# A twelve-stage decoder on one core: two mixtures of experts in eight batches of four token tiles instead of four batches of eight

## The reference, cut to what matters

```python
# layer 1: softmax router, top 2 of 8, plus a shared MLP
def _mlp(x, w1, b1, w2, b2):
    h = jax.nn.gelu(jnp.einsum('bsd,di->bsi', x, w1) + b1)
    return jnp.einsum('bsi,id->bsd', h, w2) + b2
...
# layer 3: the same without the shared MLP; the two gates are the
# softmax over the two best logits; an expert has room for 1280 tokens
```

## Time and profile before

| what | before |
|---|---|
| median of 3 runs | 2355.95 us (2353.13 to 2364.38) |
| the profiled execution's own time | 2360.56 us |
| its span, first to last instruction | 2358.8 us |
| mean granted TensorE clock | 0.854 |
| PE / DVE / ACT / POOL busy | 76% / 57% / 47% / 31% of the span |
| f1, first instruction to the phase behind it | 996.8 to 1288.5 us |
| f3, first instruction to the end | 2066.4 to 2358.8 us |

### The profile page before, as it was taken

The page is one execution under the profiler, slowest core; times in us unless marked ns, Lnnn a source line. Parts: engine busy times, 40 slices in busy tenths (PEclk is TensorE's granted clock), DMA queues, the critical chain, the costliest instruction groups (busy, mean ns, idle before and its releaser), DMA issues. The chain is left out here.

```text
span 2358.8 us, 39307 instructions
## 1 busy us (share of the span) xinstructions
PE 1786.9 (76%) x14513; PEld 1229.5 (52%) x14513; DVE 1350.3 (57%) x3525; ACT 1103.6 (47%) x2265; POOL 730.6 (31%) x617
## 2 busy tenths in 40 slices
PE   3887562899987986778994886888788778851994
PEld 1554441545544664555994553655455535551774
DVE  2888578512235764554343467974399789851223
ACT  3676440333345766633442345763366566610441
POOL 1223201270463221155453003221222132156453
PEclk9888785699997998879997787999798878855997
DMA  4111272136615001112674001000000010012224
GB/s 152 82 83 83 86 246 58 28 98 165 177 48 213 33 2 55 29 38 99 213 236 154 1 1 36 29 10 10 3 2 2 2 45 24 6 40 69 64 80 137
DMA packets 143729, 173.18 MB, mean 73 GB/s; under 512 B 20913, under 2 KB 118897, under 8 KB 142609
## 3 DMA queue, kind: packets, MB, share of 16 engines
q1 hardware_dynamic: 123956, 129.09, 17.4%
q0 software_dynamic: 13248, 28.21, 3.5%
q10 hardware_dynamic: 6336, 13.37, 1.5%
HBM read 126.84 MB, written 79.05 MB: 87 GB/s over the span
## 5 line engine op out<-in xcount | busy, mean ns | idle before, releaser
L2770 POOL DMA_INDIRECT f_back<-f_ys,f_row x158 | 151.2, 957 | 173.7 <-DVE f_ys L2931 144.4
L871 PE MATMUL a_AV<-a_vx,a_pT 128*64 128x18 f32 (+1 forms) x3072 | 115.0, 223 | 42.3 <-DVE a_att L548 16.3
L2763 POOL DMA_INDIRECT f_slots<-f_pay,f_slot x128 | 124.5, 972 | 66.0 <-issue 38.2
L871 PEld LDWEIGHTS a_AV<-a_vx,a_pT 128*64 128x64 f32 x3072 | 105.9, 146 | 71.1 <-issue 36.7
L733 ACT ACTIVATE a_e<-a_e 128x512 f32<-128x512 f32 x192 | 110.2, 622 | 67.6 <-DVE a_e L563 67.6
L858 PE MATMUL a_TP<-ident,a_e 128*128 128x128 f32 x768 | 110.2, 288 | 19.0 <-ACT a_e L733 18.4
L738 ACT COPY a_pT<-a_TP 128x512 f32<-128x512 f32 x192 | 103.7, 588 | 41.9 <-PE a_TP L858 41.7
L858 PEld LDWEIGHTS a_TP<-ident,a_e 128*128 128x128 f32 x768 | 91.4, 148 | 57.5 <-ACT a_e L733 45.8
L847 PE MATMUL a_S<-a_kbd,a_qT 64*64 64x512 f32 x768 | 118.3, 693 | 0.9 <-issue 0.6
L563 DVE TENSOR_TENSOR a_e<-a_S,a_mx 128x1024 f32<-128x1024 f32 x96 | 117.3, 1221 | 2.9
L560 DVE TENSOR_REDUCE a_mx<-a_S 128x16 f32<-128x1024 f32 x66 | 80.8, 1224 | 42.8 <-PE a_S L847 41.6
(11 more groups left out here) (481 smaller groups left out, 4611.8 us busy)
## 6 DMA issues: line engine op xcount, KB each, us to landing
f_wt<-in_f_ew SPq DMA_DIRECT2D x39, 584.0 KB
f_slots<-in_blank SPq DMA_DIRECT2D x1, 18576.0 KB
f_wt<-in_f_leaf SPq DMA_DIRECT2D x94, 98.0 KB, 2.0
f_pay<-f_back SPq DMA_DIRECT2D x8, 1024.0 KB, 5.6
f_xs<-f_slots SPq DMA_DIRECT2D x47, 144.0 KB
memory_x_k<-w_stage ACTq DMA_DIRECT2D x24, 256.0 KB, 3.1
f_slots<-in_blank SPq DMA_DIRECT2D x1, 5760.0 KB
f_xs<-leaf_slots SPq DMA_DIRECT2D x22, 256.0 KB, 3.6
```

What stands on the lines that cost most here:

```text
L871: last = pe.matmul(AV[64 * c:64 * c + 64, 2 * hp * W1:2 * (hp + 1) * W1], pT[:, hp, 64 * c:64 * c + 64], vx[:, g % 2, t, c, 2 * hp:2 * hp ...
L2763: pool.indirect_dma_start(out=slots[:, :], out_offset=bass.IndirectOffsetOnAxis(ap=slot[:, c, t:t + 1], axis=0), in_=pay[:, c, t, :], in_o ...
L2770: pool.indirect_dma_start(out=back[:, :], out_offset=bass.IndirectOffsetOnAxis(ap=row[:, i % RR, t:t + 1], axis=0), in_=ys[:, i % RY, t, : ...
```

## The change

`BT` becomes 4 and `NBAT` 8, for both mixtures. What follows from it:

- `choose`, `place`, `norm_stats`, `root`, the scatters, the loads back, the adds and the stores work on four tiles at a time, eight times.
- `turn_x` fills one PSUM bank for a batch and takes the two in turn. `take_turned` copies one bank.
- In f1 all eight shared blocks now stand inside the routing batches, and none behind them. This follows from the loop bounds, not from an edit.
- POOL takes the root of batch b + 3 behind the scatters of batch b, for b = 0 to 4.
- `scale` returns without work for a tile number of four or more, so the links of `choose` that carried tiles 4 to 7 carry none.

```diff
-    BT, NBAT = 8, NT // 8
+    BT, NBAT = 4, NT // 4
...
-    x_turned, xT_ready, logits = ph.counter("x_turned", 2), ph.counter("xT_ready", 2), ph.counter("logits")
+    x_turned, xT_ready, logits = ph.counter("x_turned"), ph.counter("xT_ready"), ph.counter("logits")
...
-                if b == 0:
-                    root(3)
+                if b + 3 < NBAT:
+                    root(b + 3)
...
             def scale(b, j):
-                if b >= NBAT:
+                if b >= NBAT or j >= BT:
                     return
...
             def take_turned(b):
-                for n in range(2):
-                    act.wait_ge(x_turned.sem, x_turned.after(b, n + 1))
-                    if b and not shared:
-                        act.wait_ge(logits.sem, logits.after(b - 1))
-                    act.copy(xTall[:, 2 * b + n if shared else n, :], PJ[:, n, :]).then_inc(xT_ready.sem, 1)
+                act.wait_ge(x_turned.sem, x_turned.after(b))
+                if b >= 2 and not shared:
+                    act.wait_ge(logits.sem, logits.after(b - 2))
+                act.copy(xTall[:, b if shared else b % 2, :], PJ[:, b % 2, :]).then_inc(xT_ready.sem, 1)
...
             def turn_x(b):
                 pe.wait_ge(xn_ready.sem, xn_ready.after(b))
-                for n in range(2):
-                    if b:
-                        pe.wait_ge(xT_ready.sem, xT_ready.after(b - 1, n + 1))
-                    for t in range(4):
-                        last = pe.transpose(PJ[:, n, P * t:P * t + P], pay[:, 0, BT * b + 4 * n + t, 0:P], k.ident[:, :])
-                    last.then_inc(x_turned.sem, 1)
+                if b >= 2:
+                    pe.wait_ge(xT_ready.sem, xT_ready.after(b - 2))
+                for t in range(BT):
+                    last = pe.transpose(PJ[:, b % 2, P * t:P * t + P], pay[:, 0, BT * b + t, 0:P], k.ident[:, :])
+                last.then_inc(x_turned.sem, 1)
```

More of the change, by code:

```diff
@@ L3013, in make_logits @@
                     pe.wait_ge(logits_taken.sem, logits_taken.after(b - 1))
[L3014 to L3019, removed]
+                pe.wait_ge(xT_ready.sem, xT_ready.after(b))
+                for t in range(BT):
+                    last = pe.matmul(LG[:, E * t:E * t + E], xTall[:, b if shared else b % 2, P * t:P * t + P], router[:, :],
+                                     start=True, stop=True)
                 last.then_inc(logits.sem, 1)
```

## The result

| what | before | changed |
|---|---|---|
| median | 2355.52 us (2353.13 to 2364.38, 4 runs) | 2387.60 us (2380.00 to 2390.61, 4 runs) |
| ratio, 95% interval | | 1.0116, 1.0090 to 1.0141 |
| the profiled execution | 2360.56 us | 2385.51 us |
| its span, mean granted clock | 2358.8 us, 0.854 | 2383.7 us, 0.851 |
| f1, first instruction to the next phase | 291.7 us | 323.4 us |

The change makes the kernel slower by 1.2%: 32.1 us between the medians. In the two profiles the difference is 24.95 us: +31.7 in f1, -4.4 in f3, and -2.4 over the ten phases that were not touched. Forecast were +25.5 in f1 (26.6 less 1.1) and -7.5 in f3.

A forecast was written before the change was run, and what follows sets the result against it. It took f1 to be held by a ring over DVE, ACT and PE through the shared blocks, f3 by POOL's scatters. +26.6 - 1.1 - 5.9 - 1.6 = +18.0 us, forecast 2375 us, range 2362 to 2388.

The forecast's parts named there:

- First batch, first turn: f1: four tiles' norm, router and choice give places 9 us earlier; then 13.6 us to the next batch's places.
- Second to fifth turn: f1, from one batch's places to the next through a shared block, with a later batch's norm: 17.35 us each.
- Sixth and seventh turn: f1, last two steps from places to places: 16.0 us with no norm left, 15.4 with no transposes either.
- half clock throughout: Rival, chance 0.06: PE stays at 1.2 GHz through second layer and `place`; 20 us over four of seven turns, 2394.
- the clock spares the gelus: Rival, chance 0.15: little besides the slow-clock gelu step costs time; six turns 1.2 us shorter, 7 us in all, 2366.
- End of f1: f1, last places to expert transposes: scatters, 5.2 us to transposes, 2 for weights; experts start 26.6 us later in all.
- weights in the way: f1's end: first four weight loads stand ahead of the slots in SP's queue; between 0 and 4.04 us, taken as 2.
- f3's first scatter: f3's start: fewer tiles bring POOL's first scatter 8.9 us forward from 24.35 us; bounds 4.9 and 12.2.
- Roots: f3: five smaller roots among POOL's scatters at 0.9 us each, 4.6, replace one of 1.59; net 3.0 us more.
- f3's adding back: f3's end: last batch's two adds at half size save 1.1 us, the smaller last store 0.5; 1.6 us less.
- the ring doesn't close: Rival, chance 0.08: DVE and ACT run ahead, POOL paces f1 at 11.0 us a turn; 2343, faster below mean turn 13.8.
- Tables: f1: gelu table load of 1.28 us in each turn, without a drain; four more turns carry 5.1 us of it.

The follow-up runs named there:

- experiment 1, f1 alone: Kernel before, with four-tile batches in f1 alone and f3 as before: 2494.42 us, ratio 1.0017 to the kernel before on the same chip.
- Experiment 2: Changed kernel, but ACT makes block b's gelus ahead of the Exp of batch b + 1: 2465.35 us (0.9916 of the kernel before), again 2469.70 us (0.9925).
- experiment 6: Changed kernel, but f1 ranks on logits, both gates from one Exp; gelus first, two weight loads ahead of slots: 2464.25 us, 0.9895 of the kernel before.

## Why the prediction was right, and which terms were off

Forecast 2375 us (2362 to 2388), slower; measured 2387.6: direction and mechanism right, the time 0.5% low. The change itself was sized too small: the sum said +18.0, the profiles show +24.95, and the medians lie 32.1 apart, 1.8 times the sum. The measured time lies 0.4 us inside the range, and that it does is partly luck. The terms that were mis-sized are the last two turns, the end of f1 and the adding back of f3; the 7 us between the profiles' difference and the medians' are the place of the two profiled executions among their runs.

- *First batch, first turn:* places at 14.8 where 14.7 was forecast, 13.8 for 13.6. *Second to fifth turn:* 17.35 each forecast, 69.4 in all; measured 69.3. The ring with its norm was understood.
- *Sixth and seventh turn:* 16.0 and 15.4 forecast, 17.2 and 16.6 measured, +2.4. I took the norm's 1.4 us off and let the clock be, and the slow stretch lay on the second layer (5.92 and 5.97 us for 3.84), which cost 2.1 a turn and gave 1.0 back in the first layer. The rival "half clock throughout" named the cost and the rival "the clock spares the gelus" the gain; each came in two turns, neither in the number of turns it was priced for.
- *End of f1:* transposes 8.8 us behind the last scatter, where 5.2 and 2 for the weights were forecast: the term **weights in the way**, 2 us, was near 3.6 here; the two experiments with two loads ahead gave 1.2 and 2.75 us back, counted from the last scatter, so four loads are worth some 2.4 to 5.5 if the cost goes by their number, which no run shows. Its upper bound of 4.04 held.
- *DVE free to copy at once*, -1.1: measured -0.7. *Adding back in f1*, -1.1: measured -1.9, but the expert part took 2.1 us more. Of this the first `hide` is 1.5: behind 11.43 us without work PE ran it at a granted clock of 0.54, 3.5 us for 2.0 at full clock before. 0.6 stays unexplained.
- *f3's first scatter:* -8.9, as forecast. *Roots:* +3.7 for +3.0. Experts -4.9 for -5.9. POOL did not wait for slots.
- *f3's adding back*, -1.6: measured -0.15, from the last scatter of results to the end (24.02 us before, 23.87 now); the experts ahead of it took 0.7 more, unexplained. This step failed: I made the last batch's adds shorter, but that stretch is bounded by the DMA engines (349 GB/s), not by DVE. The window of before would have shown it.
- *The rivals.* That the ring doesn't close was the way to a faster kernel, decided at a mean turn of 13.8. The measured mean of 16.7 was above it; with gelus ahead of the Exp it is 14.0, and that kernel was faster than before on the chip where it ran.
- *Tables.* Turns 2 to 7 show the load of 1.28 us with 0.02 and 0.01 us around it, and turns 2 to 5 came out to the sum with that price. The Trainium skill, "ScalarE: Activation LUTs", section "What ACT_TABLE_LOAD costs", would add 1.38 us of drain to each switch; no row here shows it. Its section "Table sets: the hidden batching unit" speaks against such a change, and the time agrees in sign. Experiment 2 refines it for this kernel: two loads more, placed where ACT has slack, and the experts of f1 start 18 to 20 us earlier.

What stays open: where the result was measured the kernels of experiments 2 and 6 were not run. f1 of the changed kernel has the same turns on both kinds of chip; if that held for experiment 2 as well, its experts would start at about 132 where the kernel before has 119.5, and it would still lose some 8 us there. So "faster" is shown only where the kernel before itself is slowed.

## What to carry to other kernels

Halving a batch pays where an engine's queue paces the stage and only its start-up shrinks (f3: POOL, 9 us earlier); it costs where each batch drags along work of fixed size through a ring of engines (f1: 17.3 us a turn for a block that takes 8.2 alone), so count what a turn holds that does not halve. When a loop bound changes, look for second loops that it feeds: here it pulled four free-standing blocks into the ring. And before crediting a shorter last step, read from the window whether the transfer beside it is the bound.

## What the hardware showed that I had not expected

- The same program took 2355 us in the result's runs and 2487 to 2491 on two numbered chips, and f1 of the kernel before took 31 us of that. 13.8 of them show as 17 gaps of the "issue" kind on PE that the first trace hasn't, 12.1 in `place` of batches 1 and 2; 8.2 more are DVE's late instruction in the third turn. Instruction queue bytes are the same (q8: 118 packets, 1.93 MB in both traces), and the mean granted clock is 0.854 and 0.837. Why instructions come late there is not settled, nor why the changed kernel's f1 is spared. PE waits about 5 us for ACT in each of its turns 2 to 5, which could let instructions gather, but no run here isolated that.
- A gain of 1.4 us in one engine's work can be mostly taken back by the clock: in the two turns without a norm the 1.2 GHz stretch lay on the layer without slack and cost 1.0 us net each. It can lie there in a turn with a norm as well (experiment 1, f1 alone), so the shorter wait alone doesn't explain it.
- Loading a table costs the kernel by its place. With 15 loads instead of 13 experiment 2's kernel is 16 us faster than the changed kernel on the same chip (2469.70 for 2486.11), and in the rows shown ACT waits for PE behind each load.
